# Leaf masks of three decision trees: from a TensorE product to masks copied by DMA and multiplied by VectorE

## The chip, the cores and the metric

The kernel runs on 1 core of one Trainium2 chip. The metric is the device time of one execution in microseconds (us); before the change it was measured in 3 runs. A profile comes from one execution more, which has a time of its own.

## The reference, cut to what matters

The program is a small perceiver: several attention and feed-forward stages over `x` (1024 tokens of 256) and a context. The change is in the last stage alone, in which three hard decision trees (named q, k and v) read the normalised tokens, and a softmax attention over groups of 64 tokens takes their outputs as queries, keys and values. One tree:

```python
def _fff(x, node_w, node_b, w1, b1, w2, b2):
    cur = jnp.zeros((N,), jnp.int32)
    for _ in range(DEPTH):                                   # DEPTH = 4
        score = jnp.einsum('nd,nd->n', xf, node_w[cur]) + node_b[cur]
        cur = 2 * cur + 1 + (score >= 0).astype(jnp.int32)
    sel = jax.nn.one_hot(cur - N_NODES, N_LEAVES)            # 16 leaves
    hidden_all = jax.nn.relu(jnp.einsum('nd,ldh->lnh', xf, w1) + b1[:, None, :])   # 64 columns a leaf
    hidden = hidden_all * sel.T[:, :, None]
    out = jnp.einsum('lnh,lho->no', hidden, w2) + sel @ b2
```

All 16 leaves of a tree are computed for all tokens (1024 hidden columns in all), and the hidden values of leaves that a token doesn't reach are set to zero.

## The kernel before, in words

Each engine runs its own instruction stream in order and waits on semaphores (`wait_ge(sig(name), n)`); the order of work is written out by hand. The last stage is `phase_tail`. It holds hidden columns on the 128 partitions (two leaves of 64 to a block) and tokens along the free axis. The work list (L2344) has 48 items n = (tree j, half c of the tokens, block h of hidden columns), 16 to a tree: 3 trees x 2 halves of 512 tokens x 8 blocks.

Ahead of the list the tokens are normalised and turned (L2466, L2636, L2734); every node of the three trees is scored (L2473), compared (`decide`, L2724), and a small product (L2479) with a 0.5 threshold behind it (`reach`, L2730) gives `leafT`: on partition 32j + l, 1 where the token reaches leaf l of tree j, and 0 elsewhere.

For each item:
- TensorE, `first(n)` (L2485): 6 products of 128x512 (L2495), since weights and tokens are each split in a high and a low part and 3 of the 4 combinations are taken for 2 halves of the depth, and a 7th (L2499) of `member` with `leafT`, which adds -1e30 to the hidden values of leaves that are not reached. They go to PSUM bank n % 4.
- ScalarE (L2659): `ownH` = relu(bank + b1), rounded to the product's format.
- VectorE: `own` = relu(bank + b1) (L2777), then `ownL` = own - ownH (L2782).
- TensorE, `second(n)` (L2502) or `second_rows(n)` for the last tree (L2519): 6 products of 128x512 (L2515) or 12 of 128x256 (L2537), with the tree's bias products (L2510, L2530) at h = 0.

TensorE's order is first(0), first(1), and then for every n first(n + 2), second(n). The bank of item n is free for first(n + 4) when `ownH` and `own` of item n are done. `first` of a new tree waits until its weights are split (L2489).

The weights of a tree (2 MB) come in one DMA on SyncE's queue (L2378) into one of two slots of `raw`. The weights of tree 1 and 2 are asked for one behind the other when the token halves `xL` and the node scores are done. In ScalarE's stream the splitting of the next tree's weights (`split_weights`, L2603 to L2608: `wH`, four pieces) stands behind items 3, 6, 11 and 14 of the current tree (SPLITS, L2640), and GpSimd makes `wL` from each (L2412). ScalarE also makes `member` from `leaf_raw` (L2629), and GpSimd clears `leaf_raw` (L2387). `b2_raw` and `leaf_raw` come by small DMAs (L2362, L2364).

Of the kernel before, what the change touches and what calls it, by code (L numbers as in the profile page):

```python
# [14 lines left out]
F32 = mybir.dt.float32  # L15
# [9 lines left out]
P = 128  # L25
N = B * L
# [2249 lines left out]
def phase_tail(core, x, drams, out):  # L2276
# [3 lines left out]
    with ExitStack() as ctx:  # L2280
# [9 lines left out]

        wsqT = core.tensor(ctx, "e_wsqT", [P, KD, D])
        gw = core.tensor(ctx, "e_gw", [P, KD, D])
        half = core.tensor(ctx, "e_half", [P, D])
        amp = core.tensor(ctx, "e_amp", [P, KD])
        wfeats = core.tensor(ctx, "e_wfeats", [P, KD, D])

# [6 lines left out]
        nodeb = core.tensor(ctx, "f_nodeb", [TREES * NNODE, 1])  # L2303
        leaf_raw = core.tensor(ctx, "f_leaf_raw", [P, TREES, HC * P])
        b2_raw = core.tensor(ctx, "f_b2_raw", [LEAVES, 3 * D])
        leafT = core.tensor(ctx, "f_leafT", [P, N], F32R)
        member = core.tensor(ctx, "f_member", [P, TREES, HC * P], F32R)
        own = core.tensor(ctx, "f_own", [P, 2, HALF])
# [14 lines left out]
        def leaves(j):  # L2323

            return slice(32 * j, 32 * j + NLEAF)
# [28 lines left out]
        @block.sync  # L2354
        def _(sp):
            sp.dma_start(core.packs["pe"][:, :], drams["pe"]).then_inc(sig("e_params_in"), 16)
            sp.dma_start(core.packs["pf"][:, :], drams["pf"]).then_inc(sig("f_params_in"), 16)
            sp.dma_start(nodeb[:, :], drams["pg"][0:1, 0:NN].rearrange("o n -> n o")).then_inc(sig("f_nodeb_in"), 16)
            sp.wait_ge(sig("f_clear"), 2)
            for j in range(TREES):  # L2360
                rows = min(32, LEAVES - 32 * j)
                sp.dma_start(b2_raw[32 * j:32 * j + rows, D:2 * D], drams["pg"][0:rows, NN + j * D:NN + (j + 1) * D])\  # L2362
                  .then_inc(sig("f_leaf_in"), 16)
                sp.dma_start(leaf_raw[32 * j:32 * j + rows, j, :], drams["pg"][0:rows, NN + TREES * D:NN + TREES * D + HC * P])\  # L2364
                  .then_inc(sig("f_leaf_in"), 16)
            for j in range(TREES):
                if j == 1:
                    sp.wait_ge(sig("f_paths"), 9)
                    sp.wait_ge(sig("f_path_clear"), 1)
                    for t in range(TREES):  # L2370
                        sp.dma_start(path[t * NNODE:(t + 1) * NNODE, leaves(t)],
                                     paths[:, 0:NNODE * NLEAF].rearrange("p (n l) -> p n l", n=NNODE))\
                          .then_inc(sig("f_path"), 16)
                    sp.wait_ge(sig("f_xL"), 2 * KD)
                    sp.wait_ge(sig("f_node_ps"), 2)
                elif j > 1:
                    sp.wait_ge(sig("f_wL"), 4 * (j - 1))
                sp.dma_start(raw[:, j % 2, :], drams["trees"][j]).then_inc(sig(f"f_raw_in{j % 2}"), 16)  # L2378
            for i in range(NT // 2):
                sp.wait_ge(sig("f_x"), i + 1)  # L2380
                sp.dma_start(out[:, 2 * i:2 * i + 2, :], x[:, 2 * i:2 * i + 2, :]).then_inc(sig("x_out"), 16)
            sp.wait_ge(sig("x_out"), 16 * (NT // 2))

        @block.gpsimd
        def _(pool):
            pool.memset(b2_raw[:, :], 0.0).then_inc(sig("f_clear"), 1)
            pool.memset(leaf_raw[:, :, :], 0.0).then_inc(sig("f_clear"), 1)  # L2387
            pool.memset(path[:, :], 0.0).then_inc(sig("f_path_clear"), 1)
# [44 lines left out]
        def _(pe):  # L2433
# [47 lines left out]
            pe.wait_ge(sig("f_xL"), 2 * KD)  # L2481
            pe.wait_ge(sig("f_member"), TREES)
            pe.wait_ge(sig("f_b2L"), 1)

            def first(n):  # L2485
# [4 lines left out]
                if n >= 4:  # L2490
                    pe.wait_ge(sig("f_ownH"), n - 3)
                    pe.wait_ge(sig("f_own"), n - 3)
                for k in range(KD):
                    for a, b in PRODUCTS:
                        pe.matmul(ps[:, n % 4, :], w1(j, a, k, h), xT[b][:, k, cols_of(c)],  # L2495
                                  start=(k == 0 and (a, b) == PRODUCTS[0]), stop=False)
                if n < 2:
                    pe.wait_ge(sig("f_leafT"), 2)
                pe.matmul(ps[:, n % 4, :], member[:, j, h * P:(h + 1) * P], leafT[:, cols_of(c)], start=False, stop=True)\  # L2499
                  .then_inc(sig("f_hid_ps"), 1)  # L2500

# [65 lines left out]
            for n in range(len(work)):  # L2567
# [14 lines left out]
                else:  # L2582
                    second(n)
            pe.wait_ge(sig("f_ownH"), len(work))
            pe.wait_ge(sig("f_own"), len(work))
# [7 lines left out]
        def _(act):  # L2593
            norm_scalar(act, sig, "e_ln", scratch)
            act.wait_ge(sig("e_amp"), 1)
            for c in range(2):
                act.wait_ge(sig("e_xnT_ps"), 2 * c + 1)
                act.activation(xnT[:, 0, cols_of(c)], ps[:, 2 * c, :], ACT.Copy).then_inc(sig("e_xnT_a"), 1)
                act.activation(sqT[:, 0, cols_of(c)], ps[:, 2 * c, :], ACT.Square).then_inc(sig("e_sqT_a"), 1)
            act.wait_ge(sig("f_leaf_in"), 32 * TREES)  # L2600
            act.activation(b2[0][:, :], b2_raw[:, :], ACT.Copy).then_inc(sig("f_b2H"), 1)
# [25 lines left out]
            features(3)  # L2627
            for j in range(TREES):
                act.activation(member[:, j, :], leaf_raw[:, j, :], ACT.Copy).then_inc(sig("f_member"), 1)  # L2629
            for c in range(2):  # L2630
# [24 lines left out]
            for n, (j, c, h) in enumerate(work):  # L2655
                act.wait_ge(sig("f_hid_ps"), n + 1)
                if n >= 3:
                    act.wait_ge(sig("f_second_ps"), n - 2)
                act.activation(ownS[0][:, n % 3, :], ps[:, n % 4, :], ACT.Relu, bias=b1[:, j, h:h + 1])\  # L2659
                   .then_inc(sig("f_ownH"), 1)  # L2660
# [18 lines left out]
        def _(dve):  # L2679
# [92 lines left out]

            for n, (j, c, h) in enumerate(work):
                dve.wait_ge(sig("f_ownH"), n + 1)
                if n >= 2:
                    dve.wait_ge(sig("f_ownL"), n - 1)
                dve.tensor_scalar(own[:, n % 2, :], ps[:, n % 4, :], b1[:, j, h:h + 1], 0.0, ALU.add, ALU.max)\  # L2777
                   .then_inc(sig("f_own"), 1)
                dve.wait_ge(sig("f_own"), n + 1)
                if n >= 3:  # L2780
                    dve.wait_ge(sig("f_second_ps"), n - 2)
                dve.tensor_tensor(ownS[1][:, n % 3, :], own[:, n % 2, :], ownS[0][:, n % 3, :].bitcast(F32),  # L2782
                                  ALU.subtract).then_inc(sig("f_ownL"), 1)
                for step, i in SOFT_AT.get(n, ()):
                    softmax(step, i)
# [7 lines left out]
def perceiver(nc, drams, out):  # L2793
    with ExitStack() as ctx:
        core = Core(nc, ctx)
        drams["row_stds"] = nc.dram_tensor("row_stds_dram", (B, NC * P), F32, kind="Internal").ap()
        drams["queries"] = nc.dram_tensor("queries_dram", (2 * B, 2, P, P), F32, kind="Internal").ap()
        x = core.tensor(ctx, "x", [P, NT, D])
# [130 lines left out]
```

## Time and profile before

| | us |
|---|---|
| median of 3 runs | 1558.7 (1554.46 to 1559.08) |
| the profiled execution, its own time | 1556.74 |
| its span in the trace | 1554.9 |
| `phase_tail` in it | 1334.9 to 1554.9 |
| its list of 48 items on TensorE | 1386.5 to 1548.0 |

The profile names groups of instructions by source line and engine: PE is TensorE's products, PEld its weight loads, DVE is VectorE, ACT ScalarE, POOL GpSimd, SP SyncE, and SPq the DMAs that SyncE issues. Products overlap in TensorE's pipeline, so that the duration of one is longer than the interval from one to the next; the chain of waits shows the intervals.

### The profile page before, as it was taken

Reading aid. Unit: us, or ns where it says so; the run is one execution under the profiler, and the core shown is the slowest. Engines: PE = TensorE matmul, PEld = TensorE weight load, DVE = VectorE, ACT = ScalarE, POOL = GpSimd, SP = SyncE. Lnnn points to the kernel's source line nnn. Section 1 sums busy time; section 2 is a strip of 40 time slices with the busy share of each in tenths; the row PEclk is TensorE's granted clock in tenths of the full one; section 3 lists DMA queues with packets and bytes.
Section 4 is the critical chain, followed back from the end, with each engine's and each line's share of the span. In section 5 each row is a group of like instructions: output and inputs, shape, how many; then the busy total and the mean of one; then the engine's idle time right before and its main releaser. Section 6 shows DMA issues by size and latency. Waiting matters only on the chain. (4 is left out here: it accounts for less than half of the span.)

```text
span 1554.9 us, 29202 instructions
## 1 busy us (share of the span) xinstructions
PE 1381.7 (89%) x11246; PEld 1116.2 (72%) x11246; DVE 1013.6 (65%) x2069; ACT 643.8 (41%) x1164; POOL 675.0 (43%) x576
## 2 busy tenths in 40 slices
PE   7899668669938999999999999999999994789998
PEld 4555455458936888888888888888888863457787
DVE  6599755643274687777777787777776643554444
ACT  3465212212014455555555555555555422233322
POOL 0133000010024597777877778777886431222200
PEclk9999788579968999999999999999999955899999
DMA  9798025004226688777887778877675432220000
GB/s 373 306 420 325 37 103 211 1 0 139 78 85 159 171 224 208 200 172 202 229 204 195 181 203 228 204 196 181 177 186 130 93 76 54 85 108 1 1 1 28
DMA packets 92007, 240.11 MB, mean 154 GB/s; under 512 B 13626, under 2 KB 61066, under 8 KB 89178
## 3 DMA queue, kind: packets, MB, share of 16 engines
q1 hardware_dynamic: 90142, 217.80, 49.9%
q10 hardware_dynamic: 1728, 20.45, 3.3%
q8 instruction: 90, 1.47, 0.4%
q14 instruction: 47, 0.39, 0.1%
HBM read 152.96 MB, written 6.40 MB: 102 GB/s over the span
## 5 line engine op out<-in xcount | busy, mean ns | idle before, releaser
L2148 DVE TENSOR_REDUCE d_top<-psum 128x1 f32<-128x400 f32 (+2 forms) x512 | 285.4, 573 | 81.8 <-PE psum L1782 73.2
L1678 POOL TENSOR_TENSOR d_ring<-d_ring 128x512 f32<-128x512 f32 x224 | 287.3, 1283 | 63.3 <-ACT d_ring L1965 45.4
L1965 ACT ACTIVATE d_ring<-psum 128x512 f32<-128x512 f32 (+1 forms) x416 | 230.4, 594 | 162.4 <-PE psum L1800 136.3
L1800 PEld LDWEIGHTS psum<-d_queries,d_stack 100*128 100x128 f32 (+1 forms) x1664 | 212.2, 194 | 43.4 <-issue 26.7
L1800 PE MATMUL psum<-d_queries,d_stack 100*128 100x128 f32 (+1 forms) x1664 | 231.6, 281 | 10.3 <-DVE d_queries L2163 7.8
L1782 PE MATMUL psum<-d_stack,d_queries 96*128 96x400 f32 (+1 forms) x512 | 203.4, 400 | 5.8 <-DVE d_top L2148 3.8
L1766 PE MATMUL psum<-d_wv,d_rowsT 128*128 128x256 f32 (+1 forms) x1248 | 206.2, 282 | 0.0
L1766 PEld LDWEIGHTS psum<-d_wv,d_rowsT 128*128 128x128 f32 (+1 forms) x1248 | 192.0, 186 | 2.0 <-issue 0.5
L1607 POOL TENSOR_TENSOR d_rowsT<-d_raw,d_rowsT 128x768 fp32r<-128x768 f32 (+2 forms) x62 | 117.7, 1900 | 155.3 <-ACT d_rowsT L1936 155.3
L1756 PE MATMUL psum<-d_rowsT,d_wk 128*128 128x384 f32 (+2 forms) x768 | 159.9, 357 | 3.7 <-POOL d_rowsT L1607 2.1
L1816 PE MATMUL psum<-d_ring,d_val 128*32 128x128 f32 (+1 forms) x3328 | 147.8, 287 | 0.0
L1756 PEld LDWEIGHTS psum<-d_rowsT,d_wk 128*128 128x128 f32 x768 | 134.7, 194 | 14.3 <-DVE d_stage L2139 2.7
L2139 DVE SCALAR_TENSOR_TENSOR d_stage<-psum,d_bk,d_stage 128x384 fp32r<-128x384 f32 (+2 forms) x128 | 81.1, 633 | 76.2 <-ACT d_stage L1945 75.6
L1782 PEld LDWEIGHTS psum<-d_stack,d_queries 96*128 96x128 f32 x512 | 97.5, 192 | 34.9 <-issue 22.1
L1599 POOL TENSOR_TENSOR d_raw<-d_raw,d_rowstd 128x768 f32<-128x768 f32 (+2 forms) x62 | 114.1, 1852 | 12.0 <-DMA d_raw<-ctxT_dram 12.0
L2177 DVE TENSOR_TENSOR d_ring<-d_ring 128x512 f32<-128x512 f32 (+1 forms) x128 | 102.6, 801 | 21.8 <-ACT d_ring L1965 14.9
L1950 ACT ACTIVATE d_val<-psum 128x512 f32<-128x512 f32 x96 | 57.4, 598 | 137.9 <-PE psum L1766 137.9
L1816 PEld LDWEIGHTS psum<-d_ring,d_val 128*32 128x32 f32 (+1 forms) x3328 | 85.2, 112 | 34.5 <-issue 28.5
L1945 ACT ACTIVATE d_stage<-psum,d_bk 128x384 fp32r<-128x384 f32 (+2 forms) x128 | 76.3, 596 | 54.0 <-PE psum L1756 54.0
L2777 DVE TENSOR_SCALAR f_own<-psum,pf 128x512 f32<-128x512 f32 x48 | 36.0, 750 | 76.6 <-ACT f_ownH L2659 76.6
L2412 POOL TENSOR_TENSOR f_wL<-f_raw,f_wH 128x1024 fp32r<-128x1024 f32 x12 | 31.3, 2614 | 109.5 <-ACT f_wH L2608 109.5
L2659 ACT ACTIVATE f_ownH<-psum,pf 128x512 fp32r<-128x512 f32 x48 | 33.0, 688 | 104.9 <-PE psum L2499 104.9
(406 smaller groups left out, 2204.2 us busy)
## 6 DMA issues: line engine op xcount, KB each, us to landing
d_stack<-d_stage SPq DMA_DIRECT2D x384, 200.2 KB, 4.3
a_cT<-ctxT_dram SPq DMA_DIRECT2D x14, 1601.0 KB, 15.7
a_cR<-ctx_rows_dram ACTq DMA_DIRECT2D x12, 1664.0 KB, 10.7
moe_w<-moe_w_dram SPq DMA_DIRECT2D x16, 1024.0 KB, 10.3
d_rowstd<-row_stds_dram SPq DMA_DIRECT2D x16, 801.0 KB, 6.7
d_raw<-ctxT_dram SPq DMA_DIRECT2D x32, 384.0 KB, 7.2
d_room<-ctx_rows_dram SPq DMA_DIRECT2D x12, 896.0 KB, 6.1
d_room<-ctx_rows_dram SPq DMA_DIRECT2D x12, 768.0 KB, 5.7
```

The costliest lines, as they stand in the source:

```text
L1599: eng.tensor_tensor(raw[:, :, s0:s0 + w], raw[:, :, s0:s0 + w], rowstd[:, s0:s0 + w].unsqueeze(1).broadcast_to([P, KD, w]), ALU.mult)\
L1607: eng.tensor_tensor(rowsT[:, 1, :, s0:s0 + w], raw[:, :, s0:s0 + w], rowsT[:, 0, :, s0:s0 + w].bitcast(F32), ALU.subtract).then_inc(sig(do ...
L1678: pool.tensor_tensor(sums[:, 0, m, :], first, ring[:, slot_of(u, m, c), :], ALU.add)\
L1756: last = pe.matmul(ps[:, bank, 0:w], wk[:, a, k, j * P:(j + 1) * P], rowsT[:, c, k, s0:s0 + w], start=((k, a, c) == steps[0]), stop=((k, a ...
L1766: last = pe.matmul(ps[0:w, bank, (c % 2) * D:(c % 2 + 1) * D], rowsT[:, f, k, c * P:c * P + w], wv[:, e, k, :], start=((k, e, f) == steps[ ...
L1782: pe.matmul(ps[:, M_BANK + v % 2, 0:w], queries[0:96, m, j, :], stack[0:96, m, j, s0:s0 + w], start=True, stop=True).then_inc(sig("d_top_p ...
L1800: last = pe.matmul(ps[0:w, S_BANK + (m + c) % 2, j * P:(j + 1) * P], stack[0:STACKED, m, j, c * P:c * P + w], queries[0:STACKED, m, j, :], ...
L1816: last = pe.matmul(ps[32 * g:32 * g + 32, V_BANK + m, 0:P], val[0:w, u, c, f:f + 32], ring[0:w, slot_of(u, m, c), g * P:(g + 1) * P], star ...
L1965: act.activation(ring[0:w, slot_of(u, m, c), :], ps[0:w, S_BANK + (m + c) % 2, :], ACT.Exp)\
L2139: dve.scalar_tensor_tensor(stage[:, m, 1, s0:s0 + w], ps[:, bank, 0:w], bk[:, m:m + 1], stage[:, m, 0, s0:s0 + w].bitcast(F32), ALU.add, A ...
L2148: dve.tensor_reduce(top[:, m, v:v + 1], ps[:, M_BANK + v % 2, 0:min(w, S - s0)], X, ALU.max)\
L2177: dve.tensor_tensor(sums[0:w, 1, m, :], first, ring[0:w, slot_of(u, m, c), :], ALU.add)\
```

## The change

- The 7th product of `first(n)` goes, with `leaf_raw`, its clearing, its three DMAs and the making of `member` from it.
- `leafT` is stored to memory, one half of the tokens (80 rows of 2 KB) at a time, when `reach` has made it. From there `load_members` fills a new tile `member` (128 partitions x 2 halves x 8 blocks x 512): the row of a leaf is read 64 times, for the 64 partitions of its hidden columns. One call issues two DMAs, for partitions 0 to 63 and for 64 to 127 (`side`). For tree 0's first half there is one call for each block (16 DMAs of 128 KB), for each of the other five (tree, half) pairs one call (2 DMAs of 1 MB).
- On SyncE's queue this comes in the order: tree 0's weights, the path tile, both stores, the 16 DMAs of the first half, the 2 of the second half, and then the weights of tree 1 and tree 2; then the masks of tree 1 and 2, each pair when the last `own` that reads the place has been made.
- VectorE makes `own` = (bank + b1) x mask from the bank and `member` (`of_leaf`), one item ahead of `ownL` = max(own, 0) - ownH. ScalarE makes `ownH` = relu(own) from SBUF, behind `own`; before, VectorE's `own` waited for `ownH`.
- A bank of TensorE is free when `own` is done; items 2 and 3 wait for `leafT` as their banks held its scores.
- Four small tiles of the step ahead (`wsqT`, `gw`, `wfeats`, `half`) now lie in the second half of `member`.

```diff
--- before.py
+++ after.py
-        wsqT = core.tensor(ctx, "e_wsqT", [P, KD, D])
-        gw = core.tensor(ctx, "e_gw", [P, KD, D])
-        half = core.tensor(ctx, "e_half", [P, D])
+        member = core.tensor(ctx, "f_member", [P, 2, HC, HALF])
+        spare = member[:, 1, :, :].rearrange("p h n -> p (h n)")
+        wsqT, gw, wfeats = (spare[:, i * KD * D:(i + 1) * KD * D].rearrange("p (k n) -> p k n", k=KD) for i in range(3))
+        half = spare[:, 3 * KD * D:3 * KD * D + D]
         amp = core.tensor(ctx, "e_amp", [P, KD])
-        wfeats = core.tensor(ctx, "e_wfeats", [P, KD, D])
...
-        leaf_raw = core.tensor(ctx, "f_leaf_raw", [P, TREES, HC * P])
-        member = core.tensor(ctx, "f_member", [P, TREES, HC * P], F32R)
...
-            sp.wait_ge(sig("f_clear"), 2)
+            sp.wait_ge(sig("f_clear"), 1)
             for j in range(TREES):
                 rows = min(32, LEAVES - 32 * j)
                 sp.dma_start(b2_raw[32 * j:32 * j + rows, D:2 * D], drams["pg"][0:rows, NN + j * D:NN + (j + 1) * D])\
                   .then_inc(sig("f_leaf_in"), 16)
-                sp.dma_start(leaf_raw[32 * j:32 * j + rows, j, :], drams["pg"][0:rows, NN + TREES * D:NN + TREES * D + HC * P])\
-                  .then_inc(sig("f_leaf_in"), 16)
-            for j in range(TREES):
-                if j == 1:
-                    sp.wait_ge(sig("f_paths"), 9)
-                    sp.wait_ge(sig("f_path_clear"), 1)
-                    for t in range(TREES):
-                        sp.dma_start(path[t * NNODE:(t + 1) * NNODE, leaves(t)],
-                                     paths[:, 0:NNODE * NLEAF].rearrange("p (n l) -> p n l", n=NNODE))\
-                          .then_inc(sig("f_path"), 16)
-                    sp.wait_ge(sig("f_xL"), 2 * KD)
-                    sp.wait_ge(sig("f_node_ps"), 2)
-                elif j > 1:
-                    sp.wait_ge(sig("f_wL"), 4 * (j - 1))
+
+            def load_tree(j):
+
                 sp.dma_start(raw[:, j % 2, :], drams["trees"][j]).then_inc(sig(f"f_raw_in{j % 2}"), 16)
+
+            def store_leaves(c):
+
+                sp.wait_ge(sig("f_leafT"), c + 1)
+                sp.dma_start(drams["leaf"][:, cols_of(c)], leafT[0:LEAVES, cols_of(c)].bitcast(F32))\
+                  .then_inc(sig(f"f_leaf_out{c}"), 16)
+
+            def load_members(j, c, hs, name):
+
+                for side in range(2):
+                    first = 32 * j + 2 * hs.start + side
+                    sp.dma_start(member[64 * side:64 * side + 64, c, hs, :],
+                                 drams["leaf"][first:32 * j + 2 * hs.stop:2, cols_of(c)].partition_broadcast(64))\
+                      .then_inc(sig(name), 16)
+
+            load_tree(0)
+            sp.wait_ge(sig("f_paths"), 9)
+            sp.wait_ge(sig("f_path_clear"), 1)
+            for t in range(TREES):
+                sp.dma_start(path[t * NNODE:(t + 1) * NNODE, leaves(t)],
+                             paths[:, 0:NNODE * NLEAF].rearrange("p (n l) -> p n l", n=NNODE))\
+                  .then_inc(sig("f_path"), 16)
+            store_leaves(0)
+            store_leaves(1)
+            sp.wait_ge(sig("f_leaf_out0"), 16)
+            for h in range(HC):
+                load_members(0, 0, slice(h, h + 1), f"f_first_member{h}")
+            sp.wait_ge(sig("f_leaf_out1"), 16)
+            load_members(0, 1, slice(0, HC), "f_member_in1")
+            sp.wait_ge(sig("f_xL"), 2 * KD)
+            sp.wait_ge(sig("f_node_ps"), 2)
+            load_tree(1)
+            sp.wait_ge(sig("f_wL"), 4)
+            load_tree(2)
+            for j in range(1, TREES):
+                for c in range(2):
+                    sp.wait_ge(sig("f_own"), 2 * HC * (j - 1) + HC * (c + 1))
+                    load_members(j, c, slice(0, HC), f"f_member_in{c}")
...
-            pool.memset(leaf_raw[:, :, :], 0.0).then_inc(sig("f_clear"), 1)
...
-            pe.wait_ge(sig("f_member"), TREES)
...
-                    pe.wait_ge(sig("f_ownH"), n - 3)
                     pe.wait_ge(sig("f_own"), n - 3)
+                elif n >= 2:
+                    pe.wait_ge(sig("f_leafT"), n - 1)
                 for k in range(KD):
                     for a, b in PRODUCTS:
-                        pe.matmul(ps[:, n % 4, :], w1(j, a, k, h), xT[b][:, k, cols_of(c)],
-                                  start=(k == 0 and (a, b) == PRODUCTS[0]), stop=False)
-                if n < 2:
-                    pe.wait_ge(sig("f_leafT"), 2)
-                pe.matmul(ps[:, n % 4, :], member[:, j, h * P:(h + 1) * P], leafT[:, cols_of(c)], start=False, stop=True)\
-                  .then_inc(sig("f_hid_ps"), 1)
+                        last = pe.matmul(ps[:, n % 4, :], w1(j, a, k, h), xT[b][:, k, cols_of(c)],
+                                         start=(k == 0 and (a, b) == PRODUCTS[0]),
+                                         stop=(k == KD - 1 and (a, b) == PRODUCTS[-1]))
+                last.then_inc(sig("f_hid_ps"), 1)
...
-            act.wait_ge(sig("f_leaf_in"), 32 * TREES)
+            act.wait_ge(sig("f_leaf_in"), 16 * TREES)
...
-            for j in range(TREES):
-                act.activation(member[:, j, :], leaf_raw[:, j, :], ACT.Copy).then_inc(sig("f_member"), 1)
...
-                act.wait_ge(sig("f_hid_ps"), n + 1)
+                act.wait_ge(sig("f_own"), n + 1)
-                act.activation(ownS[0][:, n % 3, :], ps[:, n % 4, :], ACT.Relu, bias=b1[:, j, h:h + 1])\
+                act.activation(ownS[0][:, n % 3, :], own[:, n % 2, :], ACT.Relu)\
                    .then_inc(sig("f_ownH"), 1)
...
-            for n, (j, c, h) in enumerate(work):
-                dve.wait_ge(sig("f_ownH"), n + 1)
+            def of_leaf(n):
+
+                j, c, h = work[n]
+                dve.wait_ge(sig("f_hid_ps"), n + 1)
+                if j == 0 and c == 0:
+                    dve.wait_ge(sig(f"f_first_member{h}"), 32)
+                elif h == 0:
+                    dve.wait_ge(sig(f"f_member_in{c}"), 32 * (j + c))
                 if n >= 2:
                     dve.wait_ge(sig("f_ownL"), n - 1)
-                dve.tensor_scalar(own[:, n % 2, :], ps[:, n % 4, :], b1[:, j, h:h + 1], 0.0, ALU.add, ALU.max)\
-                   .then_inc(sig("f_own"), 1)
-                dve.wait_ge(sig("f_own"), n + 1)
+                    dve.wait_ge(sig("f_ownH"), n - 1)
+                dve.scalar_tensor_tensor(own[:, n % 2, :], ps[:, n % 4, :], b1[:, j, h:h + 1], member[:, c, h, :],
+                                         ALU.add, ALU.mult).then_inc(sig("f_own"), 1)
+
+            of_leaf(0)
+            for n, (j, c, h) in enumerate(work):
+                if n + 1 < len(work):
+                    of_leaf(n + 1)
+                dve.wait_ge(sig("f_ownH"), n + 1)
                 if n >= 3:
                     dve.wait_ge(sig("f_second_ps"), n - 2)
-                dve.tensor_tensor(ownS[1][:, n % 3, :], own[:, n % 2, :], ownS[0][:, n % 3, :].bitcast(F32),
-                                  ALU.subtract).then_inc(sig("f_ownL"), 1)
+                dve.scalar_tensor_tensor(ownS[1][:, n % 3, :], own[:, n % 2, :], 0.0, ownS[0][:, n % 3, :].bitcast(F32),
+                                         ALU.max, ALU.subtract).then_inc(sig("f_ownL"), 1)
...
+        drams["leaf"] = nc.dram_tensor("leaf_dram", (LEAVES, N), F32, kind="Internal").ap()
```

## Rows read from the trace of the kernel before

**Rows 1.** A stretch of the list: length, busy PE, PEld, DVE, ACT, POOL; clock, DMA.
```profile
1400.00:1420.00 20.00, 20.00 (x86) 15.69 (x85) 9.80 (x14) 6.05 (x9) 3.19 (x2) 1.00 0.00 1
```

**Rows 2.** The chain that ended last, where the list begins: start us, us, what.
```profile
1392.71 1.59 PE psum L2515 x6
1394.30 1.40 PE psum L2495 x6
1395.70 0.23 PE psum L2499
1395.93 1.38 PE psum L2515 x6
...
1404.99 1.38 PE psum L2515 x6
```

**Rows 3.** Groups of instructions by shape, last stage: busy us, mean ns of one.
```profile
L2777 DVE TENSOR_SCALAR f_own<-psum,pf 128x512 f32<-128x512 f32 x48 | 36.0, 750 | 76.6 <-ACT f_ownH L2659 76.6
L2782 DVE TENSOR_TENSOR f_ownL<-f_own,f_ownH 128x512 fp32r<-128x512 f32 x48 | 33.2, 692 | 1.6
L2659 ACT ACTIVATE f_ownH<-psum,pf 128x512 fp32r<-128x512 f32 x48 | 33.0, 688 | 104.9 <-PE psum L2499 104.9
L2751 DVE SCALAR_TENSOR_TENSOR f_raw<-psum,pf 128x512 f32<-128x512 f32 x2 | 1.4, 689 | 2.6 <-PE psum L2547 2.6
```

**Rows 4.** Timeline, the making of `leafT`, the tree requests, ScalarE's first split.
```profile
1385.98 1.27 DVE L2730 TENSOR_SCALAR f_leafT<-psum 128x512 fp32r<-128x512 f32 x2
...
1385.36 0.84 SPq L2378 DMA_DIRECT2D f_raw<-trees_dram  x2
...
1396.56 1.05 ACT L2608 ACTIVATE f_wH<-f_raw 128x1024 fp32r<-128x1024 f32 x1
```

**Rows 5.** DMA issues: out<-in, count, KB each, median us from issue to landing.
```profile
f_leaf_raw<-pg_dram SPq DMA_DIRECT2D x2, 128.0 KB, 2.3
mixed_dram<-d_val SPq DMA_DIRECT2D x4, 256.0 KB, 4.0
d_rowstd<-row_stds_dram SPq DMA_DIRECT2D x16, 801.0 KB, 6.7
f_raw<-trees_dram SPq DMA_DIRECT2D x3, 2048.0 KB, 7.9
```

**Rows 6.** Stretches of 1 us: length, TensorE clock, DMA share, GB/s.
```profile
1304.00:1305.00 1.00, 0.50 0.93 217
485.00:486.00 1.00, 1.00 0.98 199
452.00:453.00 1.00, 0.50 1.02 389
1386.00:1387.00 1.00, 1.00 1.25 246
1391.00:1392.00 1.00, 1.00 1.07 459
1396.00:1397.00 1.00, 1.00 0.73 311
```

**Rows 7.** TensorE's clock (stretches as in rows 6) and node scores (timeline).
```profile
1374.00:1375.00 1.00, 0.74 0.00 0
1381.00:1382.00 1.00, 0.84 0.00 0
...
1378.00 3.53 PE L2473 MATMUL psum<-f_raw,pf 128*45 128x512 f32 x4 [0.90 <-issue]
1383.39 1.89 PE L2473 MATMUL psum<-f_raw,pf 128*45 128x512 f32 x4 [0.83 <-ACT f_raw L2636]
```

**Rows 8.** The chain that ended last, at the change from tree 0 to tree 1.
```profile
1430.52 0.69 ACT f_ownH L2659
1431.20 0.96 ACT f_wH L2608
...
1435.03 1.67 PE psum L2495 x6
```

More of the change, by code:

```diff
@@ L2583, in _ @@
                     second(n)
-            pe.wait_ge(sig("f_ownH"), len(work))
             pe.wait_ge(sig("f_own"), len(work))
```

## The prediction

> **What bounds the kernel now.** I read the slices first. From 1386 us to the end TensorE is busy throughout: in the 20 us of [rows 1] it is busy for all 20.00 at full clock, VectorE for 9.80, ScalarE for 6.05, and no DMA moves anything. Then the chain of waits in the list of items [rows 2]: nothing but TensorE's groups stands in it. One item takes 3.01 us there (6 products of L2495 in 1.40, the mask product in 0.23, 6 of L2515 in 1.38). So the interval between products is 0.23 us, and the list ends when TensorE's products end. Third, who could be late if TensorE were quicker: an item costs VectorE 0.750 + 0.692 us and ScalarE 0.688 us [rows 3] of those 3.01. Last, the DMAs around the start of the list, since the change puts transfers there.
>
> **What the change removes.** 48 products of 0.23 us: 11.1 us of TensorE, all on the path while TensorE is the bound. An item becomes 2.78 us. The clearing of `leaf_raw` on GpSimd, its three DMAs, and the three conversions on ScalarE go too. They lie in the step ahead of the list, where TensorE's random-feature products (L2426 to L2456) and then VectorE's normalisation set the pace, and I give nothing for them. Moving four small tiles into `member` is free: they are read for the last time before the first mask is asked for.
>
> **What it adds beside other work.** VectorE makes `own` from the bank and the mask. A three-operand instruction of this size from PSUM takes 0.689 us [rows 3], and `ownL` between 0.69 and 0.75 (its two nearest rows), so VectorE stays at 1.44 of 2.78 us. An item's results are due when second(n) begins, four part-steps (1.38 + 1.40 + 1.38 + 1.40 = 5.56 us) after first(n) has ended. The new path is `own` 0.7, then the wait for first(n+1), at 2.78, because `of_leaf(n+1)` stands ahead of `ownL(n)`, then 0.7 + 0.7: done at about 4.25, so 1.3 us in hand. The softmax steps that VectorE does among items 37 to 41 (five at about 0.69 us in the worst two items) eat about 1.0 us of this. No stall, but if `own` took 0.3 us more there would be a short one.
>
> **The change of trees.** Now first(14) ends at 1430.5, `ownH` and the last piece of `wH` and `wL` follow, and first(16) begins at 1435.03 [rows 8], 4.5 us later; TensorE's own work in between is 1.38 + 1.63 + 1.38 = 4.4. After the change that work is 4.2 us, and `own` (0.7) comes ahead of `ownH`: 5.3 us. Two tree changes give back 1.1 us each, 2.2 together.
>
> **The start of the list.** `leafT`'s first half is ready about 1386.6 (L2730's pair, [rows 4]). The store of 160 KB lands in 2.3 to 4.0 us ([rows 5]: a load of 128 KB, and four stores of 256 KB that queue behind each other); I take 2.5: 1389.1. Then SyncE issues at about 0.42 us each (its two tree requests, [rows 4]), and a load of 128 KB lands in 2.3 [rows 5]: block 0's two by 1392, block 1's by 1393. VectorE needs both before `ownL(0)`, done at about 1394.4. TensorE has done first(0) to first(2) and the bias products at about 1392.0 (1392.7 in [rows 2] less three masks) and stands 2.4 us. By itself this is all that the detour through memory costs.
>
> **What is queued behind it: the weights of tree 1.** This decides the sum. Before, trees 1 and 2 are asked for at 1385.4, and the first split of tree 1, behind item 3 on ScalarE, finds its weights there [rows 4]. Now SyncE asks for them after 18 mask DMAs of 4.19 MB together, on the same queue. ScalarE's split behind item 3 waits for the whole tree, and behind it on ScalarE stands `ownH(4)`; for this `ownL(4)` on VectorE waits, and for that second(4) on TensorE, with every item after it.
>
> When does tree 1 land? The data of the first mask DMA flow at about 1390.0 (a tree's flow 0.8 us after its issue, [rows 4, 6]). The rate is the disputed number: no row shows a load from memory into 64 partitions. The nearest rows: a store from 64 partitions (`mixed_dram`, at 1304) moves 217 GB/s with the DMAs 0.93 busy, copies between 32 partitions (`d_stack`, at 485) 199, while a load to all 128 partitions in which each reads the same row (`d_rowstd` and the rows behind it, at 452) moves 389, and the trees 459 in their best us [rows 6]. A mask DMA fills 64 partitions, so I take 215 GB/s: 4.19 MB in 19.5 us, to 1409.5. Both ends: at 389, 10.8 us; for the low end, `d_rowstd`'s 0.82 MB landed in 6.7 us [rows 5], less 0.8 until data flow and 1.2 for the landing 4.7, or 174 GB/s: 24.1 us. Trees 1 and 2, 4.19 MB, flowed from 1386.2 to 1396.7 [rows 6], 5.25 us each. With some 1.2 us for the landing (between 0 and 7.9 - 0.8 - 5.25 = 1.85) tree 1 is there at 1416.0.
>
> Here two rules bear on it. The Trainium skill (SBUF — State Buffer, "Door 1: The DMA port swizzle (why `[64,N]` ≈ `[32,N]`)") says that a DMA's bandwidth goes by how many of 16 ports its partitions reach, and that partitions 0 to 63 reach one half of them and 64 to 127 the other. By that rule the mask DMAs get half of the full rate, as the 217 and 199 do. Another page (DMA: Bandwidth & Descriptors, "Anatomy of one DMA") fits a load to 128 partitions by about 2 us and its bytes at 436 GB/s; by that 4.19 MB take 9.6 us, near the first rival.
>
> Then ScalarE splits (0.96) and makes `ownH(4)` (0.69), VectorE `ownL(4)` (0.69), with waits 2.5 us: second(4) begins at 1418.5. Now it begins at 1404.99 [rows 2]: 13.5 us later. Of the saving, 7 mask products lie ahead of this stall and are swallowed by it; 41 are left, 9.5 us. The start's 2.4 us are swallowed too.
>
> **The clock.** After such a stop the clock is low. Behind the step ahead TensorE stands idle until the tokens are normalised, and the granted clock falls to half (1.2 GHz) at 1374.7; some us after it has taken work again the clock comes back, at 1381.2 [rows 7]. Within that time the four node products took 3.53 us, against 1.89 for the same at full clock [rows 7], 1.6 us lost, and other products ran beside them: I take 2.5 us (0 if the clock doesn't fall, 3.2 if all of 6.5 us is work at half clock).
>
> **Sum** against the profiled execution (1556.7 us; the median of the runs is 2.0 higher): 13.5 - 9.5 + 2.5 + 2.2 = +8.7 us, 1565.4; on the median 1567.4. I put 1566.
>
> **The rivals.** *First: the masks load at the full rate.* Speaks for it: both halves of the partitions are in turn, and if the DMA engines work on both sides at once, the rows at 389 apply. Against: copies between blocks of 32 in turn stay near 200. Tree 1 lands at 1390.0 + 10.8 + 5.25 + 1.2 = 1407.2, second(4) begins at 1409.7, +4.7 - 9.5 + 2.5 + 2.2 = -0.1: no change, 1557 to 1559. If only the 16 small ones go faster, 16 issues at 0.42 us give 6.7 instead of 9.75 us: +5.7.
>
> *Second, the faster side: the tree isn't late.* If it landed by 1403.0, second(4) would wait for its own item only: 1394.4 + 4 x 2.78 = 1405.5, +0.5 - 9.5 + 2.2 = -6.8 us, 1550 to 1552. That is what the change would give with its own transfers hidden. From 1390.0 it asks for 6.29 MB in some 12 us, over 500 GB/s, more than any us shows [rows 6], or for the tree's pieces to pass the masks on the queue.
>
> *Third: masks slower than the nearest rows.* Many engines read one row of memory at the same time, in pieces of 2 KB. At 174 GB/s tree 1 comes 4.6 us later: +13.3, 1570 to 1572; a store that lands in 4.0 us adds 1.5.
>
> **Chances.** The forecast, with its own range of +5 to +12 us: 0.64. Full rate: 0.12. Tree not late: 0.08. Slower masks: 0.16. A measurement of this kernel tells about 0.3% (4.7 us) from no change. Faster: 0.09 (the second rival and a little of the first). Same: 0.13 (the first, the low edge of the forecast). Slower: 0.78. The range goes from 1556 (the full rate) to 1573 (slower masks).
>
> **What the profile of the changed kernel would show.** TensorE's interval for `first` is 1.40 us with nothing behind it. A gap of about 2.4 us ahead of second(0). DMAs at about 215 GB/s from 1390 for 20 us, then a tree at 400. ScalarE idle for over 10 us ahead of its first L2608 of tree 1, released by the DMA of `f_raw`, and TensorE idle ahead of the fifth L2515 group, then at half clock for some us. Gaps of about 1.2 us ahead of items 16 and 32. I am wrong if the mask DMAs run well over 300 GB/s, or if ScalarE's split finds its weights.

## The result: slower, by more than forecast

| | before | changed |
|---|---|---|
| median (runs; lowest to highest), us | 1558.7 (5; 1554.46 to 1560.08) | 1570.76 (5; 1567.57 to 1573.99) |
| ratio to before | | 1.0082, 95% interval 1.0061 to 1.0103 |
| span of the profiled execution | 1554.9 | 1569.3 |
| last stage: from SyncE's first request to the end of the span | 220.0 | 234.6 |

The change was forecast at +8.7 us and measured at +12.1 by the medians. The stages ahead of the change differ by several us from run to run (the last stage begins at 1334.7 in one profile and at 1329.0 in another), so below I compare the last stage alone: it is 14.6 us longer. Each kernel has one profile. From the stage's first request to the first store of `leafT` the ten profiles that have one take 51.6 to 51.9 us; what lies behind that repeats less well (see ahead of the first experiment).

First the page of the changed kernel: busy us and share, then three groups, GpSimd's `wL` and those that replace L2777 and L2659 of [rows 3]:

```profile
span 1569.3 us, 29097 instructions
...
PE 1372.9 (87%) x11198; PEld 1109.0 (71%) x11198; DVE 1019.0 (65%) x2069; ACT 638.1 (41%) x1161; POOL 669.7 (43%) x575
...
L2436 POOL TENSOR_TENSOR f_wL<-f_raw,f_wH 128x1024 fp32r<-128x1024 f32 x12 | 28.4, 2376 | 130.2 <-ACT f_wH L2629 130.2
L2803 DVE SCALAR_TENSOR_TENSOR f_own<-psum,pf,f_member 128x512 f32<-128x512 f32 x48 | 36.0, 750 | 73.8 <-PE psum L2519 67.4
L2678 ACT ACTIVATE f_ownH<-f_own 128x512 fp32r<-128x512 f32 x48 | 30.2, 631 | 102.7 <-DVE f_own L2803 102.7
```

TensorE has 48 products fewer (11198 against 11246) and VectorE is no busier, yet the kernel is slower. The chain that ended last says why (start us, us, what; the answer to [rows 2]). The item of [rows 2] that began at 1404.99 begins at 1424.27 here:

```profile
1386.51 1.96 DMA leaf_dram<-f_leafT
...
1388.48 0.54 SPq L2377
1389.03 0.04 issue
1389.07 0.60 SPq L2377
...
1400.07 20.09 DMA f_raw<-trees_dram
1420.16 0.02 issue
1420.19 0.02 ACT f_wH L2629
...
1421.15 0.62 ACT f_ownH L2678
1421.77 0.02 issue
1421.79 2.43 DVE f_ownL L2813
1424.23 0.04 issue
1424.27 2.93 PE psum L2537 x6
1427.20 2.25 PE psum L2519 x6
1429.45 1.37 PE psum L2537 x6
```

Read it from below: TensorE's group of six products (L2537, what L2515 was) waits for VectorE's `ownL`, this for ScalarE's `ownH`, which stood behind ScalarE's first split of tree 1, which waited for the tree's DMA; and that was asked for only when SyncE had issued 18 mask DMAs. The waits give the size (who waited for whom: us in total, times, longest):

```profile
PE psum L2537 <- DVE f_ownL L2813: 19.6, 2, 16.3
ACT f_wH L2629 <- DMA f_raw<-trees_dram: 19.1, 1, 19.1
DVE f_ownL L2813 <- ACT f_ownH L2678: 15.8, 1, 15.8
DVE f_own L2803 <- DMA f_member<-leaf_dram: 5.9, 2, 5.0
PEld psum L2519 <- POOL f_wL L2436: 2.4, 2, 1.2
```

A hole is a stretch in which TensorE has nothing to run. There is one of 16.3 us and one of 3.3 us at the start; the weight loads (PEld) wait for 1.2 us at each of the two changes of trees. Of the stretches of 1 us (length, clock, DMA share, GB/s, as in [rows 6]) the first four show masks, at 158 to 223 GB/s (123 to 234 over all of them), the fifth their tail with the first bytes of the trees, and the last the trees alone. The clock falls in either hole:

```profile
1393.00:1394.00 1.00, 1.00 0.62 223
1395.00:1396.00 1.00, 0.50 0.59 186
1398.00:1399.00 1.00, 0.88 0.67 219
1403.00:1404.00 1.00, 1.00 0.94 158
1412.00:1413.00 1.00, 0.50 1.00 250
1416.00:1417.00 1.00, 0.50 1.07 459
```

### The profile page after: what moved, and what is told of

Same layout as the page of the kernel before. It is cut to its first block and busy times, and to the rows that moved or that the text cites. A ratio compares the mean times of both kernels' runs of the same rounds, so it can differ in the third digit from the quotient of the medians.

```text
span 1569.3 us, 29097 instructions
## 1 busy us (share of the span) xinstructions
PE 1372.9 (87%) x11198; PEld 1109.0 (71%) x11198; DVE 1019.0 (65%) x2069; ACT 638.1 (41%) x1161; POOL 669.7 (43%) x575
## 5 line engine op out<-in xcount | busy, mean ns | idle before, releaser
L2803 DVE SCALAR_TENSOR_TENSOR f_own<-psum,pf,f_member 128x512 f32<-128x512 f32 x48 | 36.0, 750 | 73.8 <-PE psum L2519 67.4
L2678 ACT ACTIVATE f_ownH<-f_own 128x512 fp32r<-128x512 f32 x48 | 30.2, 631 | 102.7 <-DVE f_own L2803 102.7
```

## The experiments

All are the changed kernel with one edit unless said. "Stage" is the last stage of the profiled execution, from SyncE's first request to the end of the span. Each ratio is to the kernel before as timed beside that kernel (its medians lie from 1554.7 to 1558.7 us), so the medians of two rows are not to be subtracted.

| kernel | median us | ratio to before, 95% interval | stage us | against before |
|---|---|---|---|---|
| before | | 1 | 220.0 | |
| changed | 1570.8 | 1.0082, 1.0061 to 1.0103 | 234.6 | +14.6 |
| e1 tree 1 first on the queue | 1557.4 | 1.0014, 0.9996 to 1.0031 | 222.3 | +2.3 |
| e2 last split behind item 13 | 1568.8 | 1.0087, 1.0065 to 1.0108 | 232.3 | +12.3 |
| e3 splits behind 8, 10, 12, 13 | 1550.9 | 0.9966, 0.9955 to 0.9977 | 216.0 | -4.0 |
| e4 GpSimd waits for `ownL(4)` | 1571.7 (1 run) | | 231.8 | +11.8 |
| e5 no mask transfers | 1546.2 | 0.9946, 0.9926 to 0.9966 | 211.4 | -8.6 |
| e6 masks on all 128 partitions | 1561.5 | 1.0030, 1.0009 to 1.0050 | 225.7 | +5.7 |
| e7 e6 and e3 together | 1548.9 | 0.9975, 0.9952 to 0.9998 | 212.9 | -7.1 |
| e8 tree 0 keeps the product | 1549.1 | 0.9954, 0.9935 to 0.9972 | 212.6 | -7.4 |
| e9 8 items keep the product | 1546.6 | 0.9947, 0.9931 to 0.9963 | 210.7 | -9.3 |
| e10 two blocks to a mask DMA | 1567.5 (1 run) | | 232.3 | +12.3 |

One part of the stage column belongs to no edit. In e3, e6 and e10, far behind every hole, the granted clock fell to half for between 3 and 4 us (at 1492.6, 1530.7 and 1537.0), though TensorE had been busy all through the ten us before. Each time this came within 1 us of the end of one of the last tree's two sets of eight bias products. Two groups of products there take 1.6 us longer than in the other profiles; in e3's chain they are the last two lines, which take 1.58 and 1.39 us in the changed kernel:

```profile
1490.06 2.05 PE psum L2552 x8
1492.12 2.39 PE psum L2559 x12
1494.50 2.16 PE psum L2519 x6
```

So these three stages are 1.6 us longer than their edits account for, and a difference of 1 or 2 us between two rows of the column rests on single profiles. What makes the clock fall there in some profiles and not in others isn't shown.

### Is it what stands behind ScalarE's wait? (e1, e3, e5)

e1 moves one request:

```diff
+            sp.wait_ge(sig("f_xL"), 2 * KD)
+            sp.wait_ge(sig("f_node_ps"), 2)
+            load_tree(1)
             store_leaves(0)
             store_leaves(1)
...
-            sp.wait_ge(sig("f_xL"), 2 * KD)
-            sp.wait_ge(sig("f_node_ps"), 2)
-            load_tree(1)
```

> The changed kernel with one edit: the weights of tree 1 are asked for ahead of the two stores of leafT, not behind the masks of tree 0; tree 2 stays behind them. Theory (the queue: tree 1 comes late): the tree lands by 1393 us and ScalarE's first split has nothing to wait for, the 16 us hole of TensorE at item 4 is gone. But the stores now queue behind 2.1 MB: they land at about 1393 and not 1388.5, and TensorE's hole ahead of the first L2519 group's results (second(0)) grows from 3.3 to about 7.5 us. Span 1555 to 1557 against 1569.3 of the changed kernel, no difference from the kernel before. Rival (the mask DMAs slow the engines or the new order on VectorE costs): the span stays above 1565 wherever the tree stands.

The hole at item 4 is gone: ScalarE splits right behind item 3, at 1404.50. The cost went to the start, as forecast (a hole of 8.6 us, 7.5 forecast; waits of e1: us, times, longest):

```profile
DVE f_own L2803 <- DMA f_member<-leaf_dram: 12.4, 3, 10.4
PE psum L2537 <- DVE f_ownL L2813: 8.6, 1, 8.6
```

The stores landed in 7.3 us where they took 2.1, behind the tree's bytes. The change then comes to nothing: the 11 us of products pay for a hole of 8.6 us, the low clock behind it and the changes of trees.

e3 moves no DMA, only the place of ScalarE's waits:

```diff
-            SPLITS = (3, 6, 11, 14)
+            SPLITS = (8, 10, 12, 13)
```

> The changed kernel with the splits behind items 8, 10, 12 and 13 in place of 3, 6, 11 and 14; no DMA is moved. Theory (what costs is what stands behind ScalarE's wait for tree 1): the tree still lands at about 1420, but items 4 to 8 run meanwhile; the hole of 16 us shrinks to 0.5 to 3 us ahead of item 9, the clock stays up, and the changes of trees cost nothing: span 1550 to 1553, 2 to 5 us below the kernel before. Rival (the load on the DMAs or VectorE's new order is the cost): above 1565.

ScalarE's timeline in e3:

```profile
1418.64 1.06 ACT L2629 ACTIVATE f_wH<-f_raw 128x1024 fp32r<-128x1024 f32 x1 [3.42 <-DMA f_raw<-trees_dram]
```

The tree comes at 1418.64, late as before (34.0 us after `leafT`'s first half is begun, 34.4 in the changed kernel), and ScalarE still waits 3.42 us for it, but five more items have run. 18.5 us of the stage go by this line alone, although the profile holds the 1.6 us of low clock told of above; e2 shows 2.2 of them to be the changes of trees. It is this run that shows the cause: same bytes, same queue, same late tree, and the kernel takes 0.3% less time than the one before (interval 0.2% to 0.5%).

e5 takes the transfers away, and VectorE multiplies by a tile of ones; the masking is left out of the computation:

```diff
-            store_leaves(0)
-            store_leaves(1)
...
-                    load_members(0, 0, slice(h, h + 1), f"f_first_member{h}")
...
-                dve.scalar_tensor_tensor(own[:, n % 2, :], ps[:, n % 4, :], b1[:, j, h:h + 1], member[:, c, h, :],
+                dve.scalar_tensor_tensor(own[:, n % 2, :], ps[:, n % 4, :], b1[:, j, h:h + 1], ones,
```

> The changed kernel without the stores of leafT and without any mask DMA: VectorE multiplies by a tile of ones, so that the leaves are not masked in the hidden values (this part of the computation is left out). All else, VectorE's three-operand instruction and order included, is as in the changed kernel. Theory: the removed products show in full, less the two changes of trees: 11.1 - 2.2 = 8.9 us below the kernel before, span 1546, TensorE's interval from item to item 2.78 us. Rival (VectorE's new order costs by itself): above 1550.

8.6 us below before, 8.9 forecast. VectorE's new instruction and order cost nothing that the profile shows beyond the changes of trees. In its chain an item takes 1.40 + 1.37 us and TensorE has no hole in tree 0:

```profile
1392.13 1.40 PE psum L2510 x6
1393.53 1.37 PE psum L2528 x6
1394.90 1.40 PE psum L2510 x6
```

### The changes of trees (e2)

```diff
-            SPLITS = (3, 6, 11, 14)
+            SPLITS = (3, 6, 10, 13)
```

> The changed kernel with the last piece of each tree's split behind item 13 and not 14. Theory: at each of the two changes of trees the new step of own ahead of ownH costs 1.1 us of TensorE, and nothing else stands there: span 2.2 us shorter, 1567. Rival (the switch costs nothing, the rest of the difference is in the hole at item 4): 1569, and the gaps ahead of items 16 and 32 stay.

The stage is 2.2 us shorter, and no wait of TensorE for `wL` is left among the waits of e2. (The ratio can't tell 2 us, and the stage rests on one profile of each; the waits that are gone bear the 2.2 us out.) In the changed kernel this piece of the chain answers to [rows 8], with VectorE's `own` as the new link:

```profile
1450.44 0.76 DVE f_own L2803
1451.20 0.02 issue
1451.22 0.63 ACT f_ownH L2678
1451.85 0.96 ACT f_wH L2629
...
1452.88 2.40 POOL f_wL L2436
...
1455.32 1.66 PE psum L2519 x6
```

### Why are the masks slow? (e6, e7, e10)

e6 lays the hidden columns of a block out so that partition p belongs to leaf p % 2, and so fills all partitions by one DMA (the layout of the weights and VectorE's waits, which go with it, are not shown):

```diff
-                for side in range(2):
-                    first = 32 * j + 2 * hs.start + side
-                    sp.dma_start(member[64 * side:64 * side + 64, c, hs, :],
-                                 drams["leaf"][first:32 * j + 2 * hs.stop:2, cols_of(c)].partition_broadcast(64))\
-                      .then_inc(sig(name), 16)
+                for h in range(hs.start, hs.stop):
+                    rows = drams["leaf"][32 * j + 2 * h:32 * j + 2 * h + 2, cols_of(c)]
+                    sp.dma_start(member[:, c, h, :], rows.partition_broadcast(64)).then_inc(sig(name), 16)
```

> The changed kernel with the hidden columns of a block laid out so that partition p belongs to leaf p % 2 of its two. A mask DMA then fills all 128 partitions: 8 DMAs of 256 KB for each half of each tree, in pieces of 2 KB as before, each row read 64 times as before; the same bytes in all. Theory (64 partitions at a time are what holds the rate at 200 GB/s): the masks come at 350 to 400 GB/s, tree 1 lands at about 1407 and not 1420, block 1's masks at about 1392 and not 1393.7; span 1550 to 1555. Rival (many readers of one row, or pieces of 2 KB, hold the rate): still about 200 GB/s, the span stays near 1569.

Of e6 first a stretch of 1 us in the second half of the masks, then ScalarE's timeline at its first split:

```profile
1400.00:1401.00 1.00, 1.00 1.08 414
```

```profile
1409.04 1.06 ACT L2627 ACTIVATE f_wH<-f_raw 128x1024 fp32r<-128x1024 f32 x1 [9.36 <-DMA f_raw<-trees_dram]
```

The same bytes, in the same pieces of 2 KB and from the same rows, now move at 371 to 414 GB/s once the first half is in (the first half moved at 176 to 373; I don't know why). The tree lands at 1409.0, against 1420.2. Each row still has 64 readers and the pieces are the same, so neither is the limit, and the half set of partitions is left. Two things changed beside it. A DMA now reads two rows and not one; but in the kernel before `d_rowstd`, with all 128 partitions on one row, moved at 336 to 389 GB/s (452 to 455, the first of it behind another load). And the DMAs are of 256 KB, not 128 KB or 1 MB; e10 has 256 KB on 64 partitions and stays near 200. The hole falls to 6.6 us, the stage by 8.9 us, 5.7 above before. I had said 1550 to 1555 for the span and got 1560.0: the tree came 2 us later than I said, the 1.7 us of the section on e4 stayed, and the clock fell once more, 1.6 us.

e10 takes two blocks to a DMA in the first half:

```diff
-            for h in range(HC):
-                load_members(0, 0, slice(h, h + 1), f"f_first_member{h}")
+            for h in range(0, HC, 2):
+                load_members(0, 0, slice(h, h + 2), f"f_first_member{h}")
...
```

> The changed kernel with the first half's masks in 8 DMAs of 256 KB (two blocks, 64 partitions each) in place of 16 of 128 KB. In the changed kernel these 16 were issued 0.64 us apart, which by itself gives 205 GB/s, with the DMAs only 0.6 busy. Theory (64 partitions hold the rate): about 200 GB/s still, with the DMAs 0.9 busy, tree 1 lands as before the edit, within 1 us. Rival (SyncE's issuing held the rate of the first half): the first half at 300 GB/s or more and tree 1 lands 3 us sooner.

Of e10 a stretch of the first and one of the second half of the masks, and the split:

```profile
1395.00:1396.00 1.00, 0.50 1.07 229
...
1405.00:1406.00 1.00, 1.00 1.06 197
```

```profile
1414.52 1.06 ACT L2629 ACTIVATE f_wH<-f_raw 128x1024 fp32r<-128x1024 f32 x1 [12.82 <-DMA f_raw<-trees_dram]
```

Neither theory nor rival has it alone. With the DMAs fully busy (1.03 to 1.08) 64 partitions take 197 to 231 GB/s from 1391 to 1407: that is the ceiling here, and the 300 of the rival did not come. But in the changed kernel the first half was at 0.6 busy: its 16 requests are 0.64 us apart (the chain above), 128 KB each, 205 GB/s, and so SyncE's issuing held it just under the same ceiling. From the first mask request the tree lands in 27.3 us here and in 31.7 in the changed kernel. Of these 4.4 us the busier first half explains a part. The second half ran at 123 to 234 there, uneven, and at an even 197 to 227 here. The uneven run isn't owed to the small requests ahead of it: in e8 two such DMAs of 1 MB go alone, and from 1403 to 1414 they move at 111 to 268 GB/s with the DMAs 0.7 to 1.3 busy. Why, I can't say. The stage gains only 2.3 us, since the hole at the start is 4.2 us here, the low clock lasted longer behind both holes, and the clock fell once more behind them.

e7 has the edits of e6 and e3 both:

> Both edits: masks on all 128 partitions, splits behind items 8, 10, 12 and 13. Theory: no hole at any item but the first; what is left is the detour through memory, 1.5 to 3 us: span 1547 to 1550, 5 to 8 us below the kernel before. Rival for a rate that stays at 200 GB/s: as the kernel with the splits moved alone.

Stage 212.9, the span at 1547.5. ScalarE waits for no tree; what is left is a hole of 2.7 us ahead of second(0) and the low clock behind it. Against e3 alone the ratios show no gain.

### The longer way from the tree to TensorE (e4)

The chain above has 2.43 us for `ownL` where its median is 0.68. Timeline of the changed kernel, VectorE and GpSimd:

```profile
1421.79 2.42 DVE L2813 SCALAR_TENSOR_TENSOR f_ownL<-f_own,f_ownH 128x512 fp32r<-128x512 f32 x1 [15.83 <-ACT f_ownH L2678]
...
1421.32 2.34 POOL L2436 TENSOR_TENSOR f_wL<-f_raw,f_wH 128x1024 fp32r<-128x1024 f32 x1 [52.01 <-ACT f_wH L2629]
```

GpSimd begins 0.47 us earlier and ends at 1423.66; VectorE ends 0.55 us after that.

```diff
                 for q in range(4):
+                    if j == 1 and q == 0:
+                        pool.wait_ge(sig("f_ownL"), 5)
                     pool.wait_ge(sig("f_wH"), 4 * j + q + 1)
```

> The changed kernel, but GpSimd begins the first piece of tree 1's low weights only when ownL of item 4 is done. In the changed kernel that ownL took 2.42 us and not 0.68, while GpSimd's instruction L2436 of 2.34 us ran from 0.5 us ahead of it. Theory: VectorE's instruction with two operands in SBUF was held until GpSimd's ended. Then it takes 0.68 us here and TensorE goes on 1.7 us sooner behind its hole: span about 1.7 us shorter. Rival (the 2.4 us have another cause, such as the DMA writes of tree 2): it stays at 2.4 us.

```profile
1423.17 1.06 ACT L2631 ACTIVATE f_wH<-f_raw 128x1024 fp32r<-128x1024 f32 x1 [18.66 <-DMA f_raw<-trees_dram]
...
1424.78 0.69 DVE L2815 SCALAR_TENSOR_TENSOR f_ownL<-f_own,f_ownH 128x512 fp32r<-128x512 f32 x1 [15.37 <-ACT f_ownH L2680]
```

`ownL` takes 0.69 us, and TensorE's products begin at 1425.52: from the tree's landing 2.35 us and not 4.08. The stage is 2.8 us shorter: 1.7 by this, 0.4 as the tree landed sooner behind the first store (33.3 us, not 33.7), and 0.6 as the clock was back sooner (the second group behind the hole takes 1.65 us, not 2.25). The span is no shorter (1569.9), since the stages before it were 3.4 us longer in this run. So an instruction of VectorE with two operands in SBUF waited until GpSimd's was done. The rival falls: tree 2's bytes were still coming in here too (295 GB/s in the us from 1424) while `ownL` took its 0.69 us. In the kernel before the two met as well, but with VectorE first, and there GpSimd's instruction, begun 0.2 us behind it, took 2.75 us in place of 2.4 (timeline of the kernel before):

```profile
1432.02 0.69 DVE L2782 TENSOR_TENSOR f_ownL<-f_own,f_ownH 128x512 fp32r<-128x512 f32 x1
...
1432.23 2.75 POOL L2412 TENSOR_TENSOR f_wL<-f_raw,f_wH 128x1024 fp32r<-128x1024 f32 x1 [6.30 <-ACT f_wH L2608]
```

This agrees with the Trainium skill (SBUF — State Buffer, "SBUF: two separate sides"): whichever of such a VectorE instruction and a GpSimd instruction that reads SBUF starts first has the pair of SBUF ports that the two share for its whole length, and the other is held.

### Versions that beat both kernels (e8, e9)

e8 keeps the mask product for tree 0, asks for the trees where they stood before, and the masks of trees 1 and 2 behind them; e9 keeps it for the first 8 items alone, and its tree 2 stands behind the masks of tree 0's second half. Both have the last split behind item 13. To make room `b2_raw` and a scratch tile move into `member`. The core of e9:

```diff
+                if n < HC:
+                    if n < 2:
+                        pe.wait_ge(sig("f_leafT"), 2)
+                    last = pe.matmul(ps[:, n % 4, :], product[:, h * P:(h + 1) * P], leafT[:, cols_of(c)],
+                                     start=False, stop=True)
...
             load_tree(1)
+            store_leaves(0)
+            store_leaves(1)
+            sp.wait_ge(sig("f_leaf_out1"), 16)
+            sp.wait_ge(sig("f_b2L"), 1)
+            load_members(0, 1, slice(0, HC), "f_member_in1")
             sp.wait_ge(sig("f_wL"), 4)
             load_tree(2)
```

> Tree 0 keeps its mask product on TensorE (VectorE then takes relu(bank + b1)), only trees 1 and 2 use masks by DMA; trees 1 and 2 are asked for where they were before the change, and the stores and masks behind them, on 64 partitions at a time; last split behind item 13. Theory: 32 products of 0.23 us go, 7.4 us, and every transfer is hidden behind tree 0: span 1547 to 1548. Rival (the transfers cost also when nobody waits for them): above 1552.

> As the kernel in which tree 0 keeps its mask product, but the product stays for the first 8 items alone (tree 0, first half of the tokens); 40 items take masks by DMA. Order on the queue: tree 1, both stores, masks of tree 0's second half, tree 2, masks of tree 1. Theory (only a transfer that somebody waits for costs): 40 products of 0.23 us go, 9.3 us, nothing waits; the last stage takes 211 us against 220.0 before and 212.6 with the product for the whole of tree 0. Rival (masks of tree 0's second half, behind tree 1 and at 200 GB/s, come late at item 8): a hole there and 213 us or more.

Stage 212.6 and 210.7: 7.4 us and 9.3 us below before, each just what its products left out are worth (32 and 40 times 0.23 us). So 8 and 10 MB of masks, at about half the rate of the trees, cost nothing that shows where nobody waits for them. The longest wait of TensorE's weight loads for VectorE in e9 is 0.4 us:

```profile
PEld psum L2550 <- DVE f_ownL L2830: 1.5, 4, 0.4
```

e9 has the lowest time that I ran with the whole computation: ratio 0.9947, interval 0.9931 to 0.9963. The intervals of e7 and e8 overlap it, so only the stages and the products left out put e9 ahead of e8.

## Why the prediction was right, point by point

**The number.** 1566 was said and 1570.8 measured, within the stated range of 1556 to 1573. The forecast's own part of it, +5 to +12 us, is just missed: +12.1 by the medians, +14.4 by the spans of the two profiles. By the number alone the measured time lies in the 1570 to 1572 of the third rival. What was right is the mechanism; that the range holds the time is owed to the rival's end of it. The step from the sum's 1567.4 down to 1566 had no reason.

**The products removed.** 0.23 us each and 2.78 us an item, as said; e5 (with the changes of trees added), e8 and e9 bear out 11.1, 7.4 and 9.3 us.

**The work beside it.** VectorE's `own` took 0.750 us and not 0.689, as long as the instruction it replaced; `ownL` 0.68. No run had a hole of TensorE's products at the softmax steps. I hadn't seen that `ownL` can be held to 1.9 to 2.5 us by GpSimd; away from the big hole the 1.3 us in hand mostly covered it.

**The changes of trees.** 1.1 us each was said; the weight loads wait 1.2 us at each, and e2 gives 2.2 us for both.

**The start.** TensorE idle for 2.4 us said, 3.3 measured. The store landed in 2.0 us (2.5 said) but block 0's second mask came 3.6 us after the first request and block 1's 5.3 us after it, since requests are 0.64 us apart and not 0.42 and each takes 2.8 us or more to land, where 2.3 was said. The clock fell in this hole too, which the sum had not foreseen. Both lay under the later hole, as said.

**The tree behind the masks.** Right in mechanism and place: hole ahead of second(4), released by the tree's DMA through ScalarE, VectorE. The size was short. Said: second(4) 13.5 us later than before; measured 19.5 from the same point (`leafT` begins 0.17 us earlier). Two terms were mis-sized. First the landing, 1416.0 said, 1420.2 measured: I took 215 GB/s for all masks; they moved 4.19 MB from 1389.5 to about 1411, 195 GB/s on average, and the tree landed some 9 us after that against 5.25 + 1.2. In the first three of these 9 us only 250 to 322 GB/s moved with the DMAs fully busy, the masks' last bytes among them, and the trees' 360 to 481 came only then. Why the change-over was slow isn't shown. Second the way from landing to TensorE, 2.5 us said, 4.1 measured, of which e4 shows 1.7 to be GpSimd's hold on VectorE.

**The rest of the sum.** After second(4) the kernel before takes 149.9 us, the changed one 145.0: -4.9. Said: -9.5 + 2.5 + 2.2 = -4.8. The clock's part: the first two groups behind the hole take 2.93 and 2.25 us in place of 1.38 and 1.40, so 2.4 us. The prediction puts the low clock of the kernel before at 1374.7 to 1381.2; [rows 7] give 1374.5 to 1381.3, which changes nothing.

**The rivals.** The full rate fell: 64 partitions give 197 to 231 GB/s at best over a longer stretch; e6 shows that it takes all partitions. The slower masks of 174 GB/s fell too as a rate, since the mean was 195, though the landing which that rival named (4.6 us later) is nearly the one measured (4.2 us later): its number came out by a smaller loss of rate and the slow change-over to the trees together. One of the nearest rows was misread: `mixed_dram` is four stores from 16 partitions each, every fourth of partitions 0 to 63, and not one from 64. In every order in which the tree stood behind the masks it was too late for a split behind item 3. The Trainium skill's port rule (SBUF — State Buffer, "Door 1: The DMA port swizzle (why `[64,N]` ≈ `[32,N]`)"), that the bandwidth goes by the ports which the partitions reach, holds in these runs: masks on a half of the partitions get 197 to 231 GB/s where the DMAs are evenly busy (e10) and masks on all of them 371 to 414 (e6).

## What to carry to other kernels

A transfer put on a queue is paid for by what is queued behind it: look for the next large load on the same queue, for the instruction that waits for it, and for everything that stands behind that instruction on its engine. Moving that wait five items later (one line, e3) was worth 18.5 us, 2.2 of them at the changes of trees, more than all the products that the change had removed. Work taken from the bound engine should be moved only where the transfers for it have somewhere to hide: leaving the first 8 of 48 items as they were gave 9.3 of the 11.1 us. And where a mask or constant is copied over partitions, lay the data out so that one DMA reaches all of them.

## What the runs showed of the hardware that I had not expected

- A three-operand VectorE instruction with two operands in SBUF, 0.68 us, took 1.9 to 2.5 us when a GpSimd instruction of 2.4 us had started ahead of it, and 0.69 when GpSimd was made to wait (e4).
- The requests of these masks, in which one row is read by 64 partitions, leave SyncE 0.64 us apart (0.42 us for the trees in [rows 4]), with 128 KB on 64 partitions as with 256 KB on 128 (10.5 us for 16 in e6). At 128 KB each this alone holds the rate at 205 GB/s.
- The granted clock fell to half also in the hole of 3.3 us, at 1394.8, with TensorE idle from 1391.9, and came back at 1398.2, three us after it had taken work again. Behind the hole of 16.3 us it came back at 1429.0, 4.7 us after the work had. And in e3, e6 and e10 it fell with TensorE busy throughout.
- Two loads of 1 MB to 64 partitions each, alone on the queue (e8), moved at an uneven 111 to 268 GB/s. Behind eight of 256 KB (e10) they moved at an even 197 to 227.
